# Expert tiles of a routed feed-forward: SiLU after the gate half, four tiles a loop turn, and spaced row gathers on GpSimd

## The chip, the cores and the metric

The kernel runs on one core of one Trainium2 chip. The metric is the time of one execution on the device, in microseconds. The median of three runs of the kernel before is 1096.64 us (1096.44 to 1098.18).

## What is computed

The reference is a chain of four layers over 4096 tokens of 256 features, each followed by a residual sum and a layer norm: a linear-attention layer, a quantised feed-forward, a windowed attention, and a mixture of experts. Only the last is touched:

```python
scores = softmax(xt @ Wr)                      # 8 experts, xt: tokens x 256
topk_w, topk_idx = top_k(scores, 2); topk_w /= topk_w.sum()
g = silu(einsum('th,ehd->etd', xt, Wg)); u = einsum('th,ehd->etd', xt, Wu)
out_all = einsum('etd,edh->eth', g * u, Wd)    # hidden width 512
out = sum(out_all[topk_idx, tok] * topk_w) + silu(x @ Sg) * (x @ Su) @ Sd
```

The kernel computes only the two chosen experts of each token. With the inputs that the reference draws, the experts get 1063, 698, 1016, 1056, 1166, 846, 884 and 1463 rows. Cut into tiles of 128 rows these are 9, 6, 8, 9, 10, 7, 7 and 12 tiles, 68 in all; the kernel always runs NE = 71 tiles, numbered 0 to 70. The first tile of the fourth expert (number 3 when one counts from 0, as the code does) is therefore tile 9 + 6 + 8 = 23, and that of the fifth is tile 32.

## The kernel before

The program is written by hand for each engine, with semaphores between them. The layers run one after the other, with the edges overlapped. The expert tiles take about 606 to 983 us of the span; after them come the gathers of the expert outputs and the rest of the shared expert.

**TensorE** (`tile`, line 2274) does for tile i: read the place of tile i from a table in SBUF into a register (`place_of`, line 2271, a register load; the place says which expert, and in which of three SBUF slots its weights lie); transpose the hidden rows of tile i-1 (`h_transpose_e`, line 2256, recorded as L2260, four 128x128 transposes); wait until the weights of the expert are split (`w_ready`, line 2282); the gate half and the up half of tile i (`gate_up_e`, twelve matmuls of 512 columns, six for each half, since each float32 product is done as three: lines 1857 to 1859); transpose the token rows of tile i+1 (L2244); the down product of tile i-1 (`down_e`, twelve matmuls of 256 columns). All twelve matmuls of gate and up are told by one increment of `e_gu`. Tiles 5 to 66 run in a hardware loop of two tiles a turn (line 2312), the others are written out. The first tile of a turn reads two places, its own and that of the tile before.

**ScalarE** (line 806 on) does for tile i: copy the transposed hidden rows of tile i-1 (`heh`, L789), SiLU of the gate half (`gs`, L784), copy the transposed rows of tile i+1 (`xeh`, L779), and issue the load of the rows of tile i+3 from `tokens_by_expert`; before one load in four it waits until the group with these rows has been written.

**VectorE** (line 1808 on): the low part of the hidden rows of i-1 (`hel`, L1798), the product of SiLU and up half (`hb`, `hidden_e`, L1794), the low part of the rows of i+1 (`xel`, L1788), and the copy of the output of i-1 (`ye`, L1806), which the SP queue stores.

**GpSimd** (line 1014 on) does three things in one written order. It gathers token rows by expert: 17 groups, group 0 with 2 tiles, groups 1 to 15 with four and group 16 with three (tiles 68 to 70). One indirect DMA fetches the 128 rows of a tile (`fetch`, L983), then `keep` writes the group before to `tokens_by_expert` (L990). It loads the weights of an expert (`load_expert`, L1009, 1536 KB), and for experts 3 and up it first waits for the tiles that used the slot. And it splits the weights of an expert into a high and a low part, either whole (`split_expert`, L967 and L969, 128x3072 each) or in 12 parts (`split_part`, 128x512, L975 and L978 in turn) between the fetches. When the last part is done, `w_ready` rises. The weights of experts 0 and 1 are split by ScalarE and VectorE before.

The order is: fetch tiles 0 to 5; load expert 2; groups 0 and 1; groups 2 to 7 with the parts of expert 2, one part after every second fetch; group 8; load expert 3; group 9; wait for that load; groups 10 and 11 with a part of expert 3 after every fetch (eight parts); groups 12 and 13 with a part after every second fetch (four parts); groups 14 to 16; load expert 4; then whole splits. The gathers of the expert outputs at the end (L1043) each have a 128x28 sum behind them (L1047, `pause`) in six of the eight chunks.

Of the kernel before, what the change touches and what calls it, by code (L numbers as in the profile page):

```python
# [8 lines left out]
ALU = mybir.AluOpType  # L9
# [3 lines left out]
P = 128  # L13
# [27 lines left out]
E = 8  # L41
EH = 512
EW = 2 * KD * EH + EH // P * D
SLOT = 2 * EW
NE = 2 * NT + E - 1
TOKEN_0 = T // 2
DIRECT = 6
GROUPS = ((DIRECT, 8),) + tuple((i, min(i + 4, NE)) for i in range(8, NE, 4))
# [19 lines left out]
def wait(eng, sem, n):  # L68

    if not isinstance(n, int) or n > 0:  # L70
        eng.wait_ge(sem, n)
# [22 lines left out]
def build(nc, cst, xT, x, wqkvgT, wave_cols, bias_cols, coupling_rows, woutT, bout, wgu_rows, wd_rows, wqk_T, wo_rows, bo, wr, experts, out):  # L94
    ctx = ExitStack()
    with ctx:
        place = {"at": 0, "top": 0}

        def sb(name, shape, dt=F32):
            size = 2 if dt in (BF16, F16) else 4  # L100
            for s in shape[1:]:
                size *= s
            t = nc.alloc_sbuf_tensor_at(name, shape, dt, offset=base + place["at"])
            place["at"] += (size + 31) // 32 * 32
            place["top"] = max(place["top"], place["at"])
            return t
# [15 lines left out]
        zrow = sb("zrow", [P, D])  # L122
# [134 lines left out]
        ohr = sb("ohr", [P, NT * E], F32R)  # L257
# [150 lines left out]
        def _(act):  # L408
# [366 lines left out]

            def x_high_e(i, h):
                act.wait_ge(e_t, i + 1)
                wait(act, e_gu, i - 1)
                act.activation(xeh[:, h].rearrange("p a c -> p (a c)"), PS[:, h, 0:D], ACT.Copy).then_inc(e_xhi, 1)  # L779

            def silu_e(i, h):
                act.wait_ge(e_gu, i + 1)
                wait(act, e_hb, i - 1)
                act.activation(gs[:, h], PS[:, 2], ACT.Silu).then_inc(e_si, 1)  # L784

# [9 lines left out]
            def tile(i, h, groups=None, first=False, final=False):  # L795
# [3 lines left out]
                if not final:  # L799
                    x_high_e(i + 1, 1 - h)  # L800
                    if not isinstance(i, int) or DIRECT <= i + 3 < NE:
                        if groups is not None:
                            act.wait_ge(d_rows, 16 * groups)
                        rows(i + 3, 1 - h)

            x_high_e(0, 0)
            tile(0, 0, first=True)
            for i in range(1, 5):
# [18 lines left out]
            at = 4 * (NCH - 1) + 2  # L827
# [3 lines left out]
        def _(pool):  # L831
# [139 lines left out]
            def split_part(e, n):  # L971
                place_, half, cols = (e + 2) % SLOTS, n % 2, slice(n // 2 * 2 * D, (n // 2 + 1) * 2 * D)
                hi, lo, raw = (t[:, cols].rearrange("p (n d) -> p n d", d=D) for t in (hi_of[place_], lo_of[place_], raw_of[place_]))
                if half == 0:
                    pool.tensor_tensor(hi, raw, zrow[:, :].unsqueeze(1).to_broadcast([P, 2, D]), ALU.add).then_inc(high_part, 1)  # L975
                else:
                    pool.wait_ge(high_part, PARTS // 2 * (e - 2) + n // 2 + 1)
                    last_ = pool.tensor_tensor(lo, raw, hi.bitcast(F32), ALU.subtract)  # L978
                    if n == PARTS - 1:
                        last_.then_inc(w_ready, 1)  # L980

            def fetch(out_, i, done):
                pool.indirect_dma_start(out=out_, out_offset=None, in_=XD,  # L983
                                        in_offset=bass.IndirectOffsetOnAxis(ap=token_of[:, i:i + 1], axis=0)).then_inc(done, 16)

            def keep(g):
                first, end = GROUPS[g]
                pool.wait_ge(d_stage[g % 2], 16 * sum(GROUPS[n][1] - GROUPS[n][0] for n in range(g % 2, g + 1, 2)))
                wait(pool, d_rows, 16 * g)
                pool.dma_start(XS[first * P:end * P].rearrange("(n p) d -> p n d", p=P), stages[g % STAGES][:, 0:end - first]).then_inc(d_rows, 16)  # L990

            def gather_tokens(first, end, split=None, part=0, every_=2):
                for g in range(first, end):
                    if g >= STAGES:
                        pool.wait_ge(d_rows, 16 * (g - STAGES + 1))
                    for n, i in enumerate(range(*GROUPS[g])):
                        fetch(stages[g % STAGES][:, n], i, d_stage[g % 2])
                        if split is not None and n % every_ == every_ - 1:
                            split_part(split, part)
                            part += 1  # L1000
                    if g > 0:
                        keep(g - 1)

            def load_expert(e):
                if e >= SLOTS:
                    used = pool.value_load(cum_tiles[0:1, e - SLOTS:e - SLOTS + 1], min_val=1, max_val=NE)
                    pool.wait_ge(e_dn, used)
                    pool.tensor_tensor(freed[:], zrow[:, 0:4], zrow[:, 0:4], ALU.add)
                pool.dma_start(raw_of[(e + 2) % SLOTS][:], experts[e]).then_inc(d_raw2, 16)  # L1009
# [13 lines left out]
            pool.wait_ge(d_dn, 2 * AHEAD)  # L1023
            pool.wait_ge(d_raw2, 16)
            gather_tokens(2, 8, split=2)
            gather_tokens(8, 9)
            load_expert(3)
            gather_tokens(9, 10)
            pool.wait_ge(d_raw2, 16 * 2)
            gather_tokens(10, 12, split=3, every_=1)  # L1030
            gather_tokens(12, 14, split=3, part=8)
            gather_tokens(14, len(GROUPS))
            load_expert(4)
            keep(len(GROUPS) - 1)
            loaded(4)
# [41 lines left out]
        def _(dve):  # L1077
# [62 lines left out]
            for cos_, _, turns in TABLES:  # L1140
                dve.tensor_scalar(cos_[:].bitcast(U32), turns[:].bitcast(U32), 0x7FFFFFFF, None, ALU.bitwise_and).then_inc(turns_done, 1)
# [647 lines left out]
                                  xeh[:, h].rearrange("p a c -> p (a c)").bitcast(F32), ALU.subtract).then_inc(e_xlo, 1)  # L1789

            def hidden_e(i, h):
                dve.wait_ge(e_si, i + 1)
                wait(dve, e_ht, i - 1)
                dve.tensor_tensor(hb[:, h], PS[:, 3], gs[:, h], ALU.mult).then_inc(e_hb, 1)  # L1794
# [55 lines left out]
            at = 4 * last + 3  # L1850
# [3 lines left out]
        def _(pe):  # L1854
            def three(out_, wh, wl, vh, vl, first, last_):

                pe.matmul(out_, wh, vh, start=first, stop=False)  # L1857
                pe.matmul(out_, wh, vl, start=False, stop=False)  # L1858
                return pe.matmul(out_, wl, vh, start=False, stop=last_)  # L1859
# [387 lines left out]
            def gate_up_e(i, h, base_):  # L2247
                pe.wait_ge(e_xlo, i + 1)
                wait(pe, e_hb, i)
                for w in range(2):  # L2250
                    for k in range(KD):
                        at, lo = (bass.ds(base_ + i * EW + (w * KD + k) * EH, EH) for i in range(2))
                        mm = three(PS[:, 2 + w], xeh[:, h, k], xel[:, h, k], EWs[:, at], EWs[:, lo], k == 0, k == KD - 1)
                mm.then_inc(e_gu, 1)

            def h_transpose_e(i, h):
                pe.wait_ge(e_hb, i + 1)
                wait(pe, e_hlo, i - 1)
                for j in range(4):
                    t = pe.transpose(PS[:, 4 + h, j * P:(j + 1) * P], hb[:, h, j * P:(j + 1) * P], ident)  # L2260
                t.then_inc(e_ht, 1)

            def down_e(i, h, base_):
                pe.wait_ge(e_hlo, i + 1)
                wait(pe, e_y, i - 1)
                for j in range(4):
                    at, lo = (bass.ds(base_ + i * EW + 2 * KD * EH + j * D, D) for i in range(2))
                    mm = three(PS[:, 6 + h, 0:D], heh[:, h, j], hel[:, h, j], EWs[:, at], EWs[:, lo], j == 0, j == 3)
                mm.then_inc(e_dn, 1)

            def place_of(i):
                return pe.value_load(of_tile[0:1, bass.ds(i, 1)], min_val=0, max_val=SLOTS * E - 1)

            def tile(i, h, before=None, first=False, final=False):
                place = place_of(i)
                expert, at = place % E, place // E * SLOT
                if not first:
                    if before is None:
                        before = place_of(i - 1)
                        before = before // E * SLOT  # L2280
                    h_transpose_e(i - 1, 1 - h)
                pe.wait_ge(w_ready, expert + 1)
                gate_up_e(i, h, at)
                if not final:
                    x_transpose_e(i + 1, 1 - h)
                if not first:
                    down_e(i - 1, 1 - h, before)
                return at

# [16 lines left out]
            at = tile(0, 0, first=True)  # L2306
            pe.wait_ge(d_add, 2 * AHEAD)
            at = tile(1, 1, at)
            at = tile(2, 0, at)
            at = tile(3, 1, at)  # L2310
            tile(4, 0, at)
            with pe.Fori(2, (NE - 5) // 2) as r:
                at = tile(2 * r + 1, 1)
                tile(2 * r + 2, 0, at)
            at = tile(NE - 4, 1)
            for i in range(NE - 3, NE):
                at = tile(i, i % 2, at, final=i == NE - 1)
            h_transpose_e(NE - 1, 0)
            pe.wait_ge(d_xlo, AHEAD + 1)
# [92 lines left out]
```

## Time and profile before

| | us |
|---|---|
| median of 3 runs | 1096.64 |
| the profiled execution | 1101.61 |
| its span in the trace | 1099.7 |
| TensorE busy | 1032.2 (94%) |
| VectorE busy | 764.7 (70%) |
| ScalarE busy | 489.6 (45%) |
| GpSimd busy | 442.0 (40%) |

The profiled execution is one run, and 5.0 us over the median. Its span starts with the first recorded work; 1.9 us of the execution lie around it. "PE" is TensorE, "PEld" its weight loads, "PEldq" the sequencer that issues both; "DVE" is VectorE, "ACT" ScalarE, "POOL" GpSimd. A row in order of time gives the start, the duration, the engine and line, and the operation with output and inputs; the bracket behind it is how long the engine had been idle and what released it ("issue": nothing that the profile shows). The rows of one line give count, duration in ns (least, median, most) and first and last start. The chain that ended last lies on TensorE for 53% of the span.

### The profile page before, as it was taken

The numbers are of one execution on the slowest core, as the hardware profiler recorded it, in microseconds if no ns is written. First come the engines' busy times: TensorE is split into PE (matmuls) and PEld (weight loads), VectorE is DVE, ScalarE is ACT, GpSimd is POOL, SyncE is SP. The second block draws the span as 40 slices with busy tenths as digits, with TensorE's granted clock in tenths as the row PEclk, the third lists the DMA queues.
The fourth block names the chain that finished last, engine by engine and source line by source line (L and its number), as shares of the span: only waits on it lengthen the run. The fifth ranks groups of instructions, "written<-read, shape, count | busy, mean of one in ns | idle before, by whom it ended". The sixth has DMA issues, their size and how long they took to land.

```text
span 1099.7 us, 19315 instructions
## 1 busy us (share of the span) xinstructions
PE 1032.2 (94%) x5960; PEld 901.9 (82%) x5961; DVE 764.7 (70%) x1290; ACT 489.6 (45%) x914; POOL 442.0 (40%) x445
## 2 busy tenths in 40 slices
PE   6898997799999999999999999989999999999994
PEld 5676776799999998999988787878888888888883
DVE  7988998899999987787878343333444444347886
ACT  6745755774344444666751222222322222233326
POOL 1000201555544446322100787975633200018886
PEclk9999998999999999999999999999999999999997
DMA  8100000010000000311250557464413111213335
GB/s 315 70 32 20 1 29 1 1 35 1 0 0 0 0 1 1 120 40 39 64 205 6 187 172 242 141 183 160 156 52 107 56 48 54 70 58 108 123 106 191
DMA packets 41350, 87.83 MB, mean 80 GB/s; under 512 B 5970, under 2 KB 27732, under 8 KB 39892
## 3 DMA queue, kind: packets, MB, share of 16 engines
q0 software_dynamic: 9696, 35.66, 10.5%
q1 hardware_dynamic: 20804, 39.20, 10.0%
q10 hardware_dynamic: 10800, 12.32, 3.6%
q8 instruction: 29, 0.48, 0.2%
q14 instruction: 21, 0.17, 0.0%
HBM read 57.80 MB, written 29.36 MB: 79 GB/s over the span
## 4 chain that ended last, share of the span: by engine, by line
PE 53%; DVE 19%; DVEq 10%; POOL 8%; issue 5%; ACT 4%; DMA 1%; ACTq 0%; POOLq 0%
PE PS L1857 14%; PE PS L1859 13%; PE PS L1858 13%; POOL gathered L1043 6%; PE PS L2260 3%; PE PS L2012 2%; DVEq L1433 2%; DVEq L1280 2%; POOL pause L1047 1%; DVEq L1447 1%; PE PS L2244 1%; DVE hx L1292 1%; PE PS L1910 1%; DVEq L1293 1%; DVE qinv L1283 1%
## 5 line engine op out<-in xcount | busy, mean ns | idle before, releaser
L1794 DVE TENSOR_TENSOR hb<-PS,gs 128x512 f32<-128x512 f32 x71 | 49.1, 692 | 154.0 <-ACT gs L784 143.4
L1043 POOL DMA_INDIRECT gathered<-expert_outputs,pos x64 | 66.7, 1043 | 139.5 <-DMA expert_outputs<-ye 127.2
L1857 PE MATMUL PS<-EWs,xeh 128*128 x284 | 119.8, 422 | 0.0
L784 ACT ACTIVATE gs<-PS 128x512 f32<-128x512 f32 x71 | 42.5, 598 | 162.3 <-PE PS L1859 154.0
L1859 PE MATMUL PS<-EWs,xel 128*128 x284 | 112.5, 396 | 0.0
L1858 PE MATMUL PS<-EWs,xeh 128*128 x284 | 111.8, 394 | 0.0
L1857 PE MATMUL PS<-WGh,bxh 128*128 128x352 f32 x256 | 88.0, 344 | 13.4 <-DVE hv L1427 10.5
L2012 PE MATMUL PS<-WD,htf 128*128 128x256 f32 x384 | 88.5, 380 | 1.6 <-ACT htf L573 1.5
L1857 PE MATMUL PS<-EWs,heh 128*128 x284 | 85.7, 302 | 3.9 <-issue 3.9
L789 ACT ACTIVATE heh<-PS 128x512 fp32r<-128x512 f32 x71 | 42.5, 598 | 104.4 <-PE PS L2260 86.9
L1798 DVE TENSOR_TENSOR hel<-PS,heh 128x512 fp32r<-128x512 f32 x71 | 49.1, 691 | 55.0 <-ACT heh L789 46.3
L1858 PE MATMUL PS<-WGl,bxh 128*128 128x352 f32 x256 | 85.3, 333 | 0.0
L1859 PE MATMUL PS<-WGh,bxl 128*128 128x352 f32 x256 | 85.2, 333 | 0.0
L2012 PEld LDWEIGHTS PS<-WD,htf 128*128 128x128 f32 x384 | 71.2, 190 | 10.9 <-ACT htf L573 2.5
L1858 PE MATMUL PS<-EWs,heh 128*128 x284 | 80.1, 282 | 0.0
L1859 PE MATMUL PS<-EWs,hel 128*128 x284 | 80.0, 282 | 0.0
L865 POOL TENSOR_TENSOR bq<-bx,qsc 128x512 f32<-128x512 f32 x16 | 19.6, 1226 | 117.9 <-DVE bx L1294 117.9
L1857 PEld LDWEIGHTS PS<-EWs,xeh 128*128 128x128 f32 x284 | 53.9, 190 | 16.0 <-issue 0.6
L1857 PEld LDWEIGHTS PS<-WGh,bxh 128*128 128x128 f32 x256 | 50.2, 196 | 17.2 <-issue 11.9
L1859 PEld LDWEIGHTS PS<-EWs,xel 128*128 128x128 f32 x284 | 53.7, 189 | 10.5
L1858 PEld LDWEIGHTS PS<-EWs,xeh 128*128 128x128 f32 x284 | 53.9, 190 | 9.4
L1857 PEld LDWEIGHTS PS<-EWs,heh 128*128 128x128 f32 x284 | 53.5, 188 | 4.7 <-issue 4.6
(387 smaller groups left out, 3013.5 us busy)
## 6 DMA issues: line engine op xcount, KB each, us to landing
raw_of<-experts POOLq DMA_DIRECT2D x6, 1536.0 KB
expert_outputs<-ye SPq DMA_DIRECT2D x71, 128.0 KB
xe<-tokens_by_expert ACTq DMA_DIRECT2D x65, 128.0 KB
xraw<-xT SPq DMA_DIRECT2D x8, 512.0 KB, 4.1
X<-x SPq DMA_DIRECT2D x1, 4096.0 KB, 13.3
tokens<-X SPq DMA_DIRECT2D x8, 512.0 KB, 3.1
y<-X SPq DMA_DIRECT2D x7, 512.0 KB
raw_of<-experts SPq DMA_DIRECT2D x2, 1536.0 KB, 9.5
```

The lines of the kernel that those rows point to most:

```text
L784: act.activation(gs[:, h], PS[:, 2], ACT.Silu).then_inc(e_si, 1)
L789: act.activation(heh[:, h].rearrange("p a c -> p (a c)"), PS[:, 4 + h], ACT.Copy).then_inc(e_hhi, 1)
L1043: pool.indirect_dma_start(out=gathered[c][:, j, t], out_offset=None, in_=YS, in_offset=bass.IndirectOffsetOnAxis(ap=pos[:, j, 4 * c + t:4 ...
L1280: dve.drain()
L1433: dve.drain()
L1794: dve.tensor_tensor(hb[:, h], PS[:, 3], gs[:, h], ALU.mult).then_inc(e_hb, 1)
L1798: dve.tensor_tensor(hel[:, h].rearrange("p a c -> p (a c)"), PS[:, 4 + h], heh[:, h].rearrange("p a c -> p (a c)").bitcast(F32), ALU.subtr ...
L1857: pe.matmul(out_, wh, vh, start=first, stop=False)
L1858: pe.matmul(out_, wh, vl, start=False, stop=False)
L1859: return pe.matmul(out_, wl, vh, start=False, stop=last_)
L2012: mm = pe.matmul(PS[:, 7, i * D:(i + 1) * D], htf[:, i, k], WD[:, k], start=k == 0, stop=k == FT - 1)
L2260: t = pe.transpose(PS[:, 4 + h, j * P:(j + 1) * P], hb[:, h, j * P:(j + 1) * P], ident)
```

## The change

On TensorE, `e_gu` now rises twice a tile, after the gate half and after the up half; ScalarE's SiLU waits for the first, VectorE's product for the second. The transposes of the hidden rows of tile i-1 come ahead of the reading of the place of tile i, and the place of tile i-1, where it has to be read again, is read ahead of the down product. The loop takes four tiles a turn (tiles 5 to 64), and tiles 65 to 70 are written out.

On GpSimd, groups 10 to 15 all carry parts of expert 3, one after every second fetch (12 parts in 24 fetches). In groups 8, 9 and 16 each fetch is followed by a drain and a 128x128 sum of zeros. The order of groups and loads is otherwise the same.

```diff
--- before.py
+++ after.py
@@ -775,11 +775,11 @@
 
             def x_high_e(i, h):
                 act.wait_ge(e_t, i + 1)
-                wait(act, e_gu, i - 1)
+                wait(act, e_gu, 2 * i - 2)
                 act.activation(xeh[:, h].rearrange("p a c -> p (a c)"), PS[:, h, 0:D], ACT.Copy).then_inc(e_xhi, 1)
 
             def silu_e(i, h):
-                act.wait_ge(e_gu, i + 1)
+                act.wait_ge(e_gu, 2 * i + 1)
                 wait(act, e_hb, i - 1)
                 act.activation(gs[:, h], PS[:, 2], ACT.Silu).then_inc(e_si, 1)
 
@@ -989,15 +989,18 @@
                 wait(pool, d_rows, 16 * g)
                 pool.dma_start(XS[first * P:end * P].rearrange("(n p) d -> p n d", p=P), stages[g % STAGES][:, 0:end - first]).then_inc(d_rows, 16)
 
-            def gather_tokens(first, end, split=None, part=0, every_=2):
+            def gather_tokens(first, end, split=None, part=0, paced=False):
                 for g in range(first, end):
                     if g >= STAGES:
                         pool.wait_ge(d_rows, 16 * (g - STAGES + 1))
                     for n, i in enumerate(range(*GROUPS[g])):
                         fetch(stages[g % STAGES][:, n], i, d_stage[g % 2])
-                        if split is not None and n % every_ == every_ - 1:
+                        if split is not None and n % 2 == 1:
                             split_part(split, part)
                             part += 1
+                        if paced:
+                            pool.drain()
+                            pool.tensor_tensor(ohr[:, 0:P], zrow[:, 0:P], zrow[:, 0:P], ALU.add)
                     if g > 0:
                         keep(g - 1)
 
@@ -1023,13 +1026,12 @@
             pool.wait_ge(d_dn, 2 * AHEAD)
             pool.wait_ge(d_raw2, 16)
             gather_tokens(2, 8, split=2)
-            gather_tokens(8, 9)
+            gather_tokens(8, 9, paced=True)
             load_expert(3)
-            gather_tokens(9, 10)
+            gather_tokens(9, 10, paced=True)
             pool.wait_ge(d_raw2, 16 * 2)
-            gather_tokens(10, 12, split=3, every_=1)
-            gather_tokens(12, 14, split=3, part=8)
-            gather_tokens(14, len(GROUPS))
+            gather_tokens(10, 16, split=3)
+            gather_tokens(16, len(GROUPS), paced=True)
             load_expert(4)
             keep(len(GROUPS) - 1)
             loaded(4)
@@ -1789,6 +1791,7 @@
                                   xeh[:, h].rearrange("p a c -> p (a c)").bitcast(F32), ALU.subtract).then_inc(e_xlo, 1)
 
             def hidden_e(i, h):
+                dve.wait_ge(e_gu, 2 * i + 2)
                 dve.wait_ge(e_si, i + 1)
                 wait(dve, e_ht, i - 1)
                 dve.tensor_tensor(hb[:, h], PS[:, 3], gs[:, h], ALU.mult).then_inc(e_hb, 1)
@@ -2251,7 +2254,7 @@
                     for k in range(KD):
                         at, lo = (bass.ds(base_ + i * EW + (w * KD + k) * EH, EH) for i in range(2))
                         mm = three(PS[:, 2 + w], xeh[:, h, k], xel[:, h, k], EWs[:, at], EWs[:, lo], k == 0, k == KD - 1)
-                mm.then_inc(e_gu, 1)
+                    mm.then_inc(e_gu, 1)
 
             def h_transpose_e(i, h):
                 pe.wait_ge(e_hb, i + 1)
@@ -2272,18 +2275,18 @@
                 return pe.value_load(of_tile[0:1, bass.ds(i, 1)], min_val=0, max_val=SLOTS * E - 1)
 
             def tile(i, h, before=None, first=False, final=False):
+                if not first:
+                    h_transpose_e(i - 1, 1 - h)
                 place = place_of(i)
                 expert, at = place % E, place // E * SLOT
-                if not first:
-                    if before is None:
-                        before = place_of(i - 1)
-                        before = before // E * SLOT
-                    h_transpose_e(i - 1, 1 - h)
                 pe.wait_ge(w_ready, expert + 1)
                 gate_up_e(i, h, at)
                 if not final:
                     x_transpose_e(i + 1, 1 - h)
                 if not first:
+                    if before is None:
+                        before = place_of(i - 1)
+                        before = before // E * SLOT
                     down_e(i - 1, 1 - h, before)
                 return at
 
@@ -2309,11 +2312,12 @@
             at = tile(2, 0, at)
             at = tile(3, 1, at)
             tile(4, 0, at)
-            with pe.Fori(2, (NE - 5) // 2) as r:
-                at = tile(2 * r + 1, 1)
-                tile(2 * r + 2, 0, at)
-            at = tile(NE - 4, 1)
-            for i in range(NE - 3, NE):
+            with pe.Fori(0, (NE - 7) // 4 - 1) as r:
+                at = tile(4 * r + 5, 1)
+                for i in range(6, 9):
+                    at = tile(4 * r + i, i % 2, at)
+            at = tile(NE - 6, 1)
+            for i in range(NE - 5, NE):
                 at = tile(i, i % 2, at, final=i == NE - 1)
             h_transpose_e(NE - 1, 0)
             pe.wait_ge(d_xlo, AHEAD + 1)
```

## Rows read from the trace of the kernel before

**Rows 1.** Busy time by stretch: PE, PEld, DVE, ACT, POOL, then PEclk, DMA share, GB/s
```profile
185.90:192.70 6.80, 6.09 (x21) 6.12 (x22) 5.88 (x6) 4.38 (x19) 0.69 (x1) 0.50 0.00 1
...
985.00:1050.00 65.00, 64.97 (x369) 56.81 (x368) 49.17 (x100) 22.74 (x35) 57.40 (x84) 1.00 0.38 115
```

**Rows 2.** TensorE in order of time, around its idle stretches
```profile
186.61 0.63 PE L1857 MATMUL PS<-WGh,bxh 128*128 128x352 f32 x1 [5.86 <-DVE hv L1427]
...
686.63 0.65 PE L2260 MATMUL PS<-C,hb 128*128 128x128 f32 x4 [1.88 <-issue]
...
688.62 0.63 PE L1858 MATMUL PS<-EWs,xeh 128*128 x1
...
731.26 0.50 PE L1857 MATMUL PS<-EWs,xeh 128*128 x1
...
737.43 0.38 PE L1857 MATMUL PS<-EWs,heh 128*128 x1 [2.92 <-issue]
```

**Rows 3.** The hidden rows' transposes (L2260), four to a tile, in four windows
```profile
L2260 PEld LDWEIGHTS PS<-C,hb x92: 137/140/145, 611.8 to 731.0; 128*128 128x128 f32 x92
...
L2260 PE MATMUL PS<-C,hb x172: 271/273/476, 611.8 to 837.3; 128*128 128x128 f32 x172
...
L2260 PEld LDWEIGHTS PS<-C,hb x145: 137/141/145, 756.0 to 938.0; 128*128 128x128 f32 x145
...
L2260 PE MATMUL PS<-C,hb x17: 271/273/275, 953.1 to 973.0; 128*128 128x128 f32 x17
```

**Rows 4.** GpSimd in order of time: groups, split parts, and the loads of experts
```profile
628.53 1.00 POOL L983 DMA_INDIRECT Hh<-tokens,token_of  x1 [0.31 <-issue]
...
634.51 1.29 POOL L978 TENSOR_TENSOR EWs<-raw_of,EWs 128x512 fp32r<-128x512 f32 x1
...
670.06 1.00 POOL L983 DMA_INDIRECT Hh<-tokens,token_of  x1 [0.30 <-issue]
...
675.76 0.59 POOL L1009 DMA_DIRECT2D raw_of<-experts  x1
...
685.67 0.97 POOL L983 DMA_INDIRECT Hl<-tokens,token_of  x1 [3.40 <-DMA raw_of<-experts]
...
721.25 1.30 POOL L978 TENSOR_TENSOR EWs<-raw_of,EWs 128x512 fp32r<-128x512 f32 x1
...
773.95 6.80 POOL L967 TENSOR_TENSOR EWs<-raw_of,zrow 128x3072 fp32r<-128x3072 f32 x1 [6.49 <-DMA raw_of<-experts]
780.98 6.79 POOL L969 TENSOR_TENSOR EWs<-raw_of,EWs 128x3072 fp32r<-128x3072 f32 x1 [0.23 <-issue]
...
837.07 0.20 POOL L1008 TENSOR_TENSOR freed<-zrow 128x4 f32<-128x4 f32 x1 [28.66 <-PE PS L1859]
```

**Rows 5.** GpSimd in order of time, 1040 us: a short sum, then a gather
```profile
1040.08 0.24 POOL L1047 TENSOR_TENSOR pause<-zrow 128x28 f32<-128x28 f32 x1
1040.47 0.97 POOL L1043 DMA_INDIRECT gathered<-expert_outputs,pos  x1 [0.16 <-issue]
```

**Rows 6.** All engines in order of time, from tile to tile at 850 us
```profile
850.17 0.39 PE L1859 MATMUL PS<-EWs,xel 128*128 x1
...
850.68 0.60 ACT L784 ACTIVATE gs<-PS 128x512 f32<-128x512 f32 x1 [2.31 <-PE PS L1859]
...
851.31 0.69 DVE L1794 TENSOR_TENSOR hb<-PS,gs 128x512 f32<-128x512 f32 x1 [2.21 <-ACT gs L784]
...
852.05 0.66 PE L2260 MATMUL PS<-C,hb 128*128 128x128 f32 x4
...
852.56 0.50 PE L1857 MATMUL PS<-EWs,xeh 128*128 x1
```

**Rows 7.** TensorE's sequencer at lines 2272 and 2282, 849.5 to 852.4 us
```profile
L2272 PEldq TENSOR_LOAD <-of_tile x1: 302/302/302, 850.3 to 850.3; - x1
L2272 PEldq SEQ_ASSERT  x1: 18/18/18, 850.9 to 850.9; - x1
...
L2282 PEldq FUSED_REGOPS  x1: 86/86/86, 852.1 to 852.1; - x1
```

## Prediction

> **What bounds the kernel now.** I read the page first (TensorE busy 94%, and most of the chain that ended last), then the busy time by stretch, then TensorE and GpSimd in order of time over the expert tiles, and last the line of the hidden rows' transposes, whose count tells which tile TensorE has reached.
>
> The transposes come four to a tile, those of tile i-1 ahead of the gate of tile i. From 756.0 to 938.0 us lie 36 tiles of 182.0 / 36 = 5.056 us; that is the pace of the loop. The written-out tiles near the end take 19.8 / 4 = 4.95 us, on rows rounded to a tenth [rows 3]. Earlier the pace is worse: 92 transposes are 23 tiles, so the group at 730.7 us is that of tile 22, and the 22 tiles from 611.8 us take 118.9 us where the pace asks 111.2. The 172nd transpose is the last of tile 42, at 837.3 us (its group began some 0.4 earlier); 16 tiles of 5.056 back, the group at 756.0 us is that of tile 26. From tile 22 to tile 26 go 25.3 us where the pace asks 20.2. So 7.7 us are lost ahead of tile 23 and 5.1 behind it. The losses are idle stretches of TensorE (1.88 and 2.92 us) and a slow clock behind them: the 512-column matmul at 688.62 us lasts 0.63 us, against the 0.39 of an ordinary one [rows 2, 6]. They fall where GpSimd's indirect DMAs follow each other. In the last stage, where a 0.24 us sum stands behind each gather, TensorE is busy for 64.97 of 65 us [rows 1, 5]. The spacing thus has a real target.
>
> **GpSimd, part by part.** The weights of expert 3 must be split before tile 23 (9 + 6 + 8 tiles come first). The counts can be checked: expert 7's load waits for the 42 tiles of the first five, and the wait ends at 837.07 us, as the last transposes of tile 42 run, behind the down product of tile 41 [rows 3, 4]. Before, the last part ends at 721.25 + 1.30 = 722.6 us, and the gate of tile 23 starts at 731.26 [rows 2, 4]. The margin is 8.7 us. The change spends it:
>
> The spaced gathers of group 8 delay expert 3's load. An unspaced fetch takes 1.00 + 0.30 us. The new 128x128 sum is not in the trace; between 0.24 us for 28 columns and 1.29 for 512 a straight line gives 0.46. The drain is between nothing and the 0.23 us idle ahead of the second whole add, which stands behind one. A spaced fetch is then 0.97 + 0.16 + 0.46 + 0.23 = 1.8 us, at least the 0.97 + 0.16 + 0.24 = 1.4 of the last stage and at most 2.2. I take 1.8, since drain and sum are both of these kinds. Four of them add 2.2 us, and the load goes out at 678.2 instead of 675.76. Before, it was in by 685.67, 9.9 us later; a load with no gathers beside it took about 7.1 (6.49 idle and 0.56 of issue). With 9.9 it is in at 688.1; group 9, spaced, ends about 687.5. So group 10 starts at 688.1 us (684.5 to 690) instead of 685.67 [rows 4, 5].
>
> From there, parts come after every second fetch. Five such groups take 670.06 - 628.53 = 41.5 us, 8.31 each, and the second part of a group ends 634.51 + 1.29 - 628.53 = 7.3 us after the group's start [rows 4]. Six groups: 5 x 8.31 + 7.3 = 48.8 us. The last part ends at 688.1 + 48.8 = **736.9 us** (733.3 to 739), 14.3 later than before.
>
> TensorE would be at tile 23 before that: at 731.26 us if nothing were gained, and some 5 us sooner if the spacing removes its idle time. It waits on `w_ready` for 5.6 to 11 us. Queued behind that wait on its one sequencer are the gate and up of tile 23, the transposes of tile 24's rows and the down product of tile 22; ScalarE, VectorE and the SP store wait for these. Everything won ahead of tile 23, by spacing or pace, is swallowed. Against before, tile 23 starts 736.9 - 731.26 = **+5.6 us** (+2.0 to +7.7).
>
> The wait also costs clock. After an idle stretch of 5.86 us TensorE ran at 0.50, the lower of its levels (1.2 instead of 2.4 GHz), for 6.8 us, in which it was busy for 6.1: some 3.0 us lost [rows 1, 2]. After 1.88 us idle, about 3.4 us were slow by the matmul durations around 688.62: 1.7 lost. Here I take **+2.4 us** (+1.0 to +3.1).
>
> Behind tile 23 the gain is real: of the 5.1 us lost between tiles 22 and 26, I take back **-4.5 us** (-2.5 to -5.1). The parts of groups 14 and 15, the spaced group 16 and the later load leave no row of bare fetches. Group 16 adds 3 x 0.5 us on GpSimd, under the split of expert 4 (load at about 745, 10 us of load, 14 of splitting: ready by 770, needed for tile 32 near 782). Its cover is 12 us; gone, each us would be one.
>
> **The tile itself.** Before, 0.51 us pass from the start of the last gate-and-up matmul to the SiLU (850.17 to 850.68), 0.63 to the product, 0.74 to the transposes and 0.51 to the next gate (852.56): 2.39 us, and the other 2.67 of the pace are the gate and up matmuls [rows 3, 6]. SiLU on the gate half takes its 0.63 us off this round: it runs beside the up half's six matmuls. But the register load moves behind the transposes. Before, the sequencer did it at 850.2 to 850.9, under the down product. It then stood at the transposes: the next register work (L2282) is stamped 852.1, the transposes' own start, not 851.0 [rows 7]. So the load cannot start ahead of the end of the transposes' wait, and the gate behind it comes 0.78 us later (about 0.1 of index, 0.30 of load, 0.4 of checks and arithmetic, 850.2 to 851.0). The round grows by 0.78 - 0.63 = 0.15, to 5.21 us. Off this come the loop's branch and second place, which stretched each second tile before and now lie between the down product and the wait, on nothing; the written-out tiles (4.95) bound what they and the loop cost together at 0.10. A second wait on VectorE may add up to 0.1, and a load that stays hidden would give 4.95. I take 5.08, a little under the middle of 4.95 and 5.3, since the loop's cost leaves for certain. Some 47 tiles follow tile 23: 47 x (5.08 - 5.056) = **+1.1 us** (-5 to +8).
>
> The load took 0.30 us here [rows 7]. The Trainium skill ("DMA: Bandwidth & Descriptors", latency and other measured facts) states a floor of about 600 ns for `tensor_load`. By that figure the exposed load would add 0.3 us a tile, 14 us more; the trace disagrees, and I go by the trace.
>
> **Sum.** 5.6 + 2.4 - 4.5 + 1.1 = +4.6 us. The terms come from one profiled execution of 1101.61 us (span 1099.7), 5.0 over the median. If part of that excess is TensorE's idle time, the gain is smaller and the wait longer in an unprofiled run, so I don't scale the sum down: 1096.64 + 4.6 = 1101.2 us.
>
> **Rivals.**
> (a) The register load stays hidden because waiting transposes don't hold the sequencer. Then the tiles run at 4.95: 47 x -0.106 = -5.0 instead of +1.1, and with the wait 5.6 + 2.4 - 4.5 - 5.0 = -1.5, 1095.1 us, no change. The stamps of rows 7 speak against it. The Trainium skill ("Advanced Engine Details and Errata", sequencer and instruction queues) speaks for it: engine instructions wait in a queue for their semaphores while others are read.
> (b) Faster: expert 3 is ready early. A fetch pitch of 1.4 and a 7 us load put the last part at 733.3 us. With (a)'s pace: 2.0 + 1.0 - 5.1 - 5.0 = -7, 1089.5 us. It is faster for any last part up to about 734.5. Against: the 9.9 us that this load took.
> (c) The spacing does not do what it says: the idle time is TensorE's own, or the load's traffic. Then nothing comes back behind tile 23: 5.6 + 2.4 + 1.1 = +9, 1105.7 us. The last stage's full TensorE speaks against, though its work is looser.
>
> **Chances.** Forecast 0.53, (a) 0.20, (b) 0.12, (c) 0.15. A change under 0.2% (2.2 us) cannot be told from none. Faster: (b) and a little of (a), 0.16. Same: most of (a) and the low end of the forecast, 0.24. Slower: 0.60. The range leaves out the ends of (b) and of (c): 1092.5 to 1107.5.
>
> **What would show it.** An idle stretch of TensorE of 6 to 11 us ahead of tile 23's gate, ended by the last L978 part near 737 us; a slow clock behind it; expert 3's load going out near 678; no idle stretch over 0.5 us elsewhere from 671 us on; L2272's load stamped behind the transposes, and the pace from 756 to 938 us at 5.03 to 5.15. I am wrong if TensorE does not wait there, or if the last part ends before 731 us.

## The result and the profile after

The changed kernel takes 1130.34 us (median of 4 runs, 1129.7 to 1131.65) against 1096.59 beside it: a ratio of 1.0302 (95% interval 1.0289 to 1.0316), 33.75 us slower. Forecast were 1101.2 us and a range of 1092.5 to 1107.5. The profiled execution took 1131.65 us, with a span of 1129.7 against 1099.7.

The page of the changed kernel, its head (busy us, share of the span, instructions):

```profile
span 1129.7 us, 19363 instructions
PE 1028.4 (91%) x5960; PEld 897.4 (79%) x5961; DVE 768.5 (68%) x1290; ACT 497.4 (44%) x914; POOL 445.9 (39%) x456
```

TensorE's work is nearly the same (1028.4 us busy, 1032.2 before); the span around it has grown. Who TensorE waited for, 560 to 1040 us (us in total, times, longest):

```profile
PE PS L1860 <- POOL EWs L978: 32.9, 1, 32.9
PE PS L1860 <- issue: 2.7, 8, 0.7
```

One wait of 32.9 us, for a split part of GpSimd. Before, no row of this view named GpSimd. In order of time, TensorE and GpSimd at its end:

```profile
758.21 1.27 POOL L978 TENSOR_TENSOR EWs<-raw_of,EWs 128x512 fp32r<-128x512 f32 x1
...
759.88 0.79 PE L1860 MATMUL PS<-EWs,xeh 128*128 x1 [32.91 <-POOL EWs L978]
760.46 0.63 PE L1861 MATMUL PS<-EWs,xeh 128*128 x1
```

This is tile 23's gate, held by expert 3's last part, which ends at 759.5 us (722.6 before, [rows 4]). The matmuls behind it last 0.63 us, as those at the low clock in [rows 2]. The stretch behind the wait (span, then busy PE, PEld, DVE, ACT, POOL, clock, DMA share, GB/s), and the transposes that follow it:

```profile
759.90:764.50 4.60, 4.60 (x11) 3.63 (x12) 0.00 (x0) 0.60 (x1) 1.33 (x2) 0.50 0.53 145
```

```profile
766.39 0.46 PEld L2263 LDWEIGHTS PS<-C,hb 128*128 128x128 f32 x4
```

The granted clock is 0.50, the lower level (1.2 instead of 2.4 GHz). Where GpSimd's time went, in order of time, from the start of group 8 to that of group 10:

```profile
669.75 1.00 POOL L983 DMA_INDIRECT Hh<-tokens,token_of  x1 [0.30 <-issue]
675.33 0.40 POOL L1003 TENSOR_TENSOR ohr<-zrow 128x128 fp32r<-128x128 f32 x1 [4.58 <-issue]
676.00 0.97 POOL L983 DMA_INDIRECT Hh<-tokens,token_of  x1 [0.28 <-issue]
678.92 0.40 POOL L1003 TENSOR_TENSOR ohr<-zrow 128x128 fp32r<-128x128 f32 x1 [1.95 <-issue]
...
688.16 0.57 POOL L1012 DMA_DIRECT2D raw_of<-experts  x1 [0.29 <-issue]
689.03 1.02 POOL L983 DMA_INDIRECT Hh<-tokens,token_of  x1 [0.30 <-issue]
696.99 0.40 POOL L1003 TENSOR_TENSOR ohr<-zrow 128x128 fp32r<-128x128 f32 x1 [6.94 <-issue]
...
710.78 1.00 POOL L983 DMA_INDIRECT Hl<-tokens,token_of  x1 [0.30 <-issue]
```

and the line of the drains (count; ns least, median, most):

```profile
L1002 POOLq DRAIN  x11: 3032/4239/9342, 666.0 to 771.8; - x11
```

The engine is idle not behind the sum but between fetch and sum: the drain does not end when the fetch has been issued. The drain's own durations say too much, because its stamp can begin ahead of the fetch: the first starts at 666.0 us and its fetch only at 669.75. What it costs is read from the idle time ahead of the eleven sums, 36.5 us together, 1.9 to 6.9 each. The longest, 6.94 us, stands behind the fetch that had the 1536 KB load of expert 3 ahead of it; the DMA engines were busy for 0.90 of the time up to that sum and 0.27 behind it:

```profile
689.00:697.00 8.00, 7.54 (x46) 6.41 (x46) 3.54 (x8) 2.18 (x4) 1.03 (x2) 1.00 0.90 299
697.00:702.00 5.00, 4.89 (x31) 4.19 (x30) 2.08 (x5) 1.59 (x3) 1.60 (x3) 1.00 0.27 66
```

The two other first fetches of a group, behind the store of a group of rows, come next (4.58 and 4.74 us). That the drain lasts until transfers are done is the reading that fits these rows; which transfers it waits for was not tested. The two spaced groups take 710.78 - 669.75 = 41.0 us, against 15.6 before and the 18.0 forecast.

The pace, in the transposes' line, for 36 tiles from tile 26's transposes on, and TensorE's sequencer at one tile:

```profile
L2263 PEld LDWEIGHTS PS<-C,hb x145: 137/141/141, 782.0 to 968.3; 128*128 128x128 f32 x145
...
L2275 PEldq TENSOR_LOAD <-of_tile x1: 302/302/302, 854.0 to 854.0; - x1
L2275 PEldq SEQ_ASSERT  x1: 18/18/18, 854.6 to 854.6; - x1
...
L2282 PEldq FUSED_REGOPS  x1: 86/86/86, 854.7 to 854.7; - x1
```

```profile
852.65 0.39 PE L1862 MATMUL PS<-EWs,xel 128*128 x1
...
853.08 0.69 DVE L1797 TENSOR_TENSOR hb<-PS,gs 128x512 f32<-128x512 f32 x1 [1.87 <-PE PS L1862]
...
854.52 0.60 PE L2263 MATMUL PS<-C,hb 128*128 128x128 f32 x4
...
855.22 0.50 PE L1860 MATMUL PS<-EWs,xeh 128*128 x1
```

The pace is 186.3 / 36 = 5.17 us (5.056 before, [rows 3]). The product starts 0.43 us behind the last matmul's start and ends at 853.77; the register load is stamped 854.0, behind it, not under the down product as in [rows 7]; the gate follows at 855.22. From the product's end to the gate are 1.45 us, with the load and its arithmetic in them; before it was 0.56 [rows 6]. From the last gate-and-up matmul's start to the gate are 855.22 - 852.65 = 2.57 us, against 2.39 before.

### The profile page after: what moved, and what is told of

Same layout as the page of the kernel before. It is cut to its first block, busy times and chain, and to the rows that moved or that the text cites. A ratio compares the mean times of both kernels' runs of the same rounds, so it can differ in the third digit from the quotient of the medians.

```text
span 1129.7 us, 19363 instructions
## 1 busy us (share of the span) xinstructions
PE 1028.4 (91%) x5960; PEld 897.4 (79%) x5961; DVE 768.5 (68%) x1290; ACT 497.4 (44%) x914; POOL 445.9 (39%) x456
## 4 chain that ended last, share of the span: by engine, by line
PE 41%; DVE 19%; POOL 14%; DVEq 10%; issue 8%; ACT 5%; DMA 1%; POOLq 1%; ACTq 0%
PE PS L1860 11%; PE PS L1862 10%; PE PS L1861 10%; POOL gathered L1045 4%; PE PS L2015 2%; PE PS L2263 2%; POOL even_rows L983 2%; DVEq L1435 2%; DVEq L1282 2%; POOL Hh L983 1%; POOL EWs L978 1%; POOL Hl L983 1%; POOL EWs L975 1%; DVEq L1449 1%; DVE hx L1294 1%
## 5 line engine op out<-in xcount | busy, mean ns | idle before, releaser
L1860 PE MATMUL PS<-EWs,xeh 128*128 x284 | 119.7, 422 | 39.8 <-POOL EWs L978 32.9
L779 ACT ACTIVATE xeh<-PS 128x256 fp32r<-128x256 f32 x71 | 27.4, 386 | 87.4 <-PE PS L2247 85.3
```

## Experiments

All kernels compute the full result. The kernel before was run beside each set, and its median is given with it, since it differs between sets: 1096.59 beside the changed kernel, 1097.56 beside the first three runs below (chip 6), 1087.64 beside the next four (chip 12) and 1088.18 beside the last four (chip 7). The kernels that wait long at tile 23 do not get those 10 us: the change without drains takes 1105.37 us on chip 12, the one without drains and sums 1104.32 on chip 6. So across sets neither times nor ratios can be compared to better than the 10 us (0.9%), and conclusions rest on kernels of one set where there are two.

**No drain and no sum.** The changed kernel with

```diff
-            gather_tokens(8, 9, paced=True)
+            gather_tokens(8, 9)
...
-            gather_tokens(9, 10, paced=True)
+            gather_tokens(9, 10)
...
-            gather_tokens(16, len(GROUPS), paced=True)
+            gather_tokens(16, len(GROUPS))
```

> The changed kernel with neither drain nor sum behind the fetches of groups 8, 9 and 16; the twelve parts stay spread over groups 10 to 15. Theory D: expert 3's load is out at 675.8 us, the last part ends at 685.7 + 48.8 = 734.5 us, TensorE waits 1 to 7 us at tile 23, and idle stretches of 1 to 3 us come back in groups 8, 9 and 16: 1102 to 1108 us. Rival S: over 1120 us. If this is faster than the run without the drain, the sum buys nothing.

1104.32 us, ratio 1.0060 (1.0043 to 1.0077). The waits of TensorE, 600 to 1000 us:

```profile
PE PS L1860 <- POOL EWs L978: 5.9, 1, 5.9
```

The spacing costs 26 of the 33.7 us, by medians of two sets in which the kernel before is within 1 us. The spread of the parts costs a wait of 5.9 us: the last part ends at 730.30 + 1.27 = 731.6 us in this trace (734.5 was given; group 8 starts 2 us earlier than assumed). Groups 8 and 9 were bare, and the idle stretches that were expected there did not come back: TensorE is busy for 49.15 of the 50 us from 670 on.

**The tiles' part alone.** The TensorE, ScalarE and VectorE hunks of the change, GpSimd's code as before.

> The TensorE, ScalarE and VectorE part of the change alone, GpSimd as before. Theory P (the register load behind the transposes lengthens each tile's round): 5.18 us from 756 to 938 us as in the changed kernel, against 5.056 before, over some 66 tiles 8 us, less what slack it gives against idle stretches: 1101 to 1106 us. Rival Q (the slower pace is GpSimd's doing, the splits or the later load): pace 5.06 or less, 1094 to 1098 us.

1100.23 us, ratio 1.0025 (1.0016 to 1.0035). The pace is P's, so it is not GpSimd's doing:

```profile
L2261 PEld LDWEIGHTS PS<-C,hb x145: 137/141/142, 750.8 to 937.0; 128*128 128x128 f32 x145
```

186.2 / 36 = 5.17 us. The time is a little under the range given, so the longer round costs less than 8 us. From the transposes of tile 0 to those of tile 22 go 115.9 us, 3.0 less than before [rows 3], although the pace is slower: less is lost to idle time there. That the longer round leaves slack for it is a guess; from tile 22 to tile 26 go 25.4 us, as before.

**The place ahead of the transposes again.** The kernel of the last run with

```diff
 def tile(i, h, before=None, first=False, final=False):
+    place = place_of(i)
+    expert, at = place % E, place // E * SLOT
     if not first:
         h_transpose_e(i - 1, 1 - h)
-    place = place_of(i)
-    expert, at = place % E, place // E * SLOT
```

> As the run before this one, but the place is read ahead of the transposes again, so that SiLU on the gate half and the four-tile loop act alone. Theory P: the register load is under the down product again, the SiLU's 0.63 us are off the round, and the tiles are bound by TensorE's own work: pace 4.95 to 4.98 us, 66 x -0.1 = 6.6 us less than before, 1088 to 1092 us. Rival Q or a bound elsewhere: pace 5.03 or more, 1095 us or more.

1080.43 us, ratio 0.9844 (0.9827 to 0.9860): 20 us less than the run above by two moved lines, and 8 us under the range given. Pace and one tile's turn in this kernel:

```profile
L2261 PEld LDWEIGHTS PS<-C,hb x145: 137/141/141, 744.0 to 917.5; 128*128 128x128 f32 x145
```

```profile
853.68 0.69 DVE L1795 TENSOR_TENSOR hb<-PS,gs 128x512 f32<-128x512 f32 x1 [1.50 <-PE PS L1860]
...
854.84 0.28 PE L1860 MATMUL PS<-EWs,hel 128*128 x1
854.96 0.49 PE L2261 MATMUL PS<-C,hb 128*128 128x128 f32 x3
```

The pace is 173.5 / 36 = 4.82 us. The product ends at 854.37, the transposes start 0.12 us behind the last down matmul: nothing but TensorE's own work sets the tile. The prediction and theory P took 4.95 for that floor; it was too high. In this trace one long stretch of idle time is left, which ends as expert 4's load goes out (736.82 us):

```profile
736.81 0.38 PE L1858 MATMUL PS<-EWs,heh 128*128 x1 [3.01 <-DVE hel L1799]
```

**Sums without drains.** The changed kernel with (a counter `spaced = [0]` is set up in front)

```diff
-    pool.drain()
-    pool.tensor_tensor(ohr[:, 0:P], zrow[:, 0:P], zrow[:, 0:P], ALU.add)
+    at = 23 * spaced[0]
+    spaced[0] += 1
+    pool.tensor_tensor(ohr[:, at:at + 23], zrow[:, 0:23], zrow[:, 0:23], ALU.add)
```

> The changed kernel with no drain; behind each fetch of groups 8, 9 and 16 stands a sum of 23 columns, each into columns of its own, instead of the 128x128 sum into one place. Theory D (the drain waits for the landing): a spaced fetch takes about 1.4 us, the load of expert 3 is out by 677, the last part ends at 734 to 737 us, TensorE waits 7 to 11 us at tile 23; 1103 to 1108 us, as without any spacing (1104.3), since what the sums win ahead of tile 23 is lost in the wait. Rival S (the sum, not the drain, costs the time): the load goes out after 682 us and the run takes over 1112 us.

1105.37 us, ratio 1.0159 (1.0142 to 1.0176). GpSimd in order of time:

```profile
671.27 0.97 POOL L983 DMA_INDIRECT Hh<-tokens,token_of  x1 [0.16 <-issue]
672.26 0.23 POOL L1006 TENSOR_TENSOR ohr<-zrow 128x23 fp32r<-128x23 f32 x1
672.65 0.97 POOL L983 DMA_INDIRECT Hh<-tokens,token_of  x1 [0.16 <-DMA tokens_by_expert<-even_rows]
```

A spaced fetch takes 672.65 - 671.27 = 1.38 us, the 1.4 of [rows 5]. The wait is 7.1 us instead of 32.9. The sum is smaller here too, 0.23 us against 0.40 in the changed kernel; that is under 2 us over the eight fetches ahead of group 10, and the rest is the drain's. No run takes out the drain and leaves the 128x128 sum.

**Sums in the faster kernel.** Place first, SiLU on the gate half, four tiles a turn, GpSimd's order of before, and behind the fetches of groups 8, 9 and 12 to 16 a sum as above, of 9 columns.

> The place read ahead of the transposes, SiLU on the gate half and four tiles a turn (1080.4 us by itself), GpSimd in the order of before, and a sum of 9 columns, with no drain, behind every fetch of groups 8, 9 and 12 to 16. Theory B (bare fetches one behind the other are what idles TensorE): the stretch of 9.0 us from transposes to transposes at 731 to 740 us goes to under 5.5, 4 to 5 us won, 1075 to 1077 us. Rival L (the idle time comes with the row loads and stores landing late while GpSimd's DMAs are in flight, whatever their spacing by a fraction of a us): the 9 us stretch stays, 1079 to 1082 us.

1078.77 us, ratio 0.9915 (0.9899 to 0.9932). The time lies between the two ranges, and it decides nothing between B and L: the stretch at 731 to 740 us is gone, but the next run, of the same set and without the sums, has none either. What the trace shows is a 5.0 us wait on expert 3's part at tile 23, longer than in the same kernel without the sums (3.4, last run but one): the last part ends at 722.5 us here and at 719.1 there.

**Two tiles a turn.** The kernel before with (the three waits on `e_gu` in short)

```diff
-                mm.then_inc(e_gu, 1)
+                    mm.then_inc(e_gu, 1)
...
-                act.wait_ge(e_gu, i + 1)
+                act.wait_ge(e_gu, 2 * i + 1)
...
+                dve.wait_ge(e_gu, 2 * i + 2)
```

and the place of tile i-1 read ahead of the down product.

> The kernel before with SiLU on the gate half and the place of the tile before read ahead of the down product; two tiles a turn and the place ahead of the transposes as before. Theory P: most of the 0.24 us a tile of the run with the place first (4.82 against 5.056) is SiLU's 0.63 us off the round, so the pace here is 4.82 to 4.86 and the time 1080 to 1083 us. Rival R: the branch every second tile sets half of it, pace 4.9 to 4.97, 1086 to 1091 us.

1078.77 us, ratio 0.9920 (0.9903 to 0.9936). The pace over 33 tiles, 754.5 to 913.5 us, is 159.0 / 33 = 4.82 us:

```profile
L2261 PEld LDWEIGHTS PS<-C,hb x133: 137/141/141, 754.5 to 913.5; 128*128 128x128 f32 x133
```

So all of the pace is there with two tiles a turn. The time is 1.2 us under the range given, which was reckoned from a set with a slower kernel before.

**GpSimd's part alone.** The GpSimd hunks on the kernel before.

> The GpSimd part of the change alone (drains, sums, spread parts), the tiles as before. Theory D: the last part ends at 759 to 760 us as in the changed kernel, TensorE waits about 30 us at tile 23, and from there the tiles go at 5.05 instead of 5.18 us: 48 x 0.13 = 6 us less than the changed kernel, 1122 to 1126 us. If the last part ends much earlier, the tiles' part delays GpSimd through shared DMA traffic.

1125.15 us, ratio 1.0344 (1.0327 to 1.0361). TensorE's waits, and the drains:

```profile
PE PS L1859 <- POOL EWs L978: 35.1, 1, 35.1
```

```profile
L1002 POOLq DRAIN  x11: 3021/4097/9567, 664.7 to 769.4; - x11
```

GpSimd's part by itself loses 37.5 us here, so it makes all of the loss. The wait is 35.1 us where about 30 were given; the last part ends at 757.1. Beside it, in the same set, the run with sums and no drains is 19.8 us faster (1105.37), although it has the slower tiles.

**Expert 3's and 4's loads earlier.** The two-tile kernel with

```diff
-            gather_tokens(2, 8, split=2)
-            gather_tokens(8, 9)
+            gather_tokens(2, 7, split=2)
             load_expert(3)
-            gather_tokens(9, 10)
+            gather_tokens(7, 8, split=2, part=10)
+            gather_tokens(8, 9)
             pool.wait_ge(d_raw2, 16 * 2)
-            gather_tokens(10, 12, split=3, every_=1)
-            gather_tokens(12, 14, split=3, part=8)
-            gather_tokens(14, len(GROUPS))
+            gather_tokens(9, 12, split=3, every_=1)
             load_expert(4)
+            gather_tokens(12, len(GROUPS))
```

> As the run with SiLU on the gate half and two tiles a turn, and expert 3's load issued after group 6 instead of 8, its twelve parts behind the fetches of groups 9 to 11, expert 4's load after group 11 instead of 16. Theory W (in the faster tiles tile 23 is held by expert 3's last part, 2.5 us in that run's trace): the last part ends before 713 us, no wait on it at tile 23, 2 to 3 us less than that run beside it on the same chip. Rival B (bare fetches behind one another idle TensorE): groups 12 to 16 are now bare, 19 fetches in a row, and give back 2 to 5 us, so that it is not faster.

1072.03 us, ratio 0.9849 (0.9832 to 0.9865), the lowest time of all runs and 5.0 us under the best other kernel of its set (1077.03, below). GpSimd's last part, and the busy time of 670 to 760 us (span, then PE, PEld, DVE, ACT, POOL, clock, DMA share):

```profile
705.31 1.31 POOL L978 TENSOR_TENSOR EWs<-raw_of,EWs 128x512 fp32r<-128x512 f32 x1
```

```profile
670.00:760.00 90.00, 90.00 (x556) 79.48 (x556) 40.32 (x74) 29.47 (x57) 71.97 (x63) 1.00 0.59 186
```

The part ends at 706.6, ahead of tile 23 at 718, and TensorE is never idle in this stretch, though 19 bare fetches follow one another. So the wait is gone, as theory W has it, and on this chip B falls. W's 2 to 3 us could not be checked: the same two-tile kernel was not run in this set, and its ratio above, 0.9920, comes from another.

**Four tiles a turn alone.** As the place-first run, with `e_gu` once a tile and SiLU behind the whole gate and up.

> The kernel before with four tiles a turn, the place of the tile before read ahead of the down product, and SiLU behind the whole gate and up as before. Theory P: the round with the whole SiLU is about 5.0 us (2.39 us from the last matmul to the gate, 2.6 of matmuls), so the pace from tile 26 to 62 is 4.95 to 5.02, and the time 0 to 6 us under before. Rival R (branch and second place cost the pace): 4.82 to 4.86.

1082.13 us, ratio 0.9937 (0.9917 to 0.9957), pace 179.8 / 36 = 4.99 us:

```profile
L2260 PEld LDWEIGHTS PS<-C,hb x145: 137/140/145, 741.0 to 920.8; 128*128 128x128 f32 x145
```

Without the earlier SiLU the larger loop and the place of the tile before take 0.06 us off the round; with it they are hidden.

**The place first once more.**

> The run with the place first and four tiles a turn once more, to stand beside the two-tile loop and the two runs before on one chip. If four tiles a turn buy nothing, pace 4.82 and the time within 2 us of the two-tile run's ratio to before.

1077.03 us, ratio 0.9898 (0.9881 to 0.9914), pace 4.82. Its interval overlaps the two-tile run's (0.9903 to 0.9936), so four tiles a turn show no clear gain. In the first set the same kernel had 0.9844: the tiles' gain was 17 us there and is 11 here. In this set the idle stretch at 731 us is not there. TensorE now waits 3.4 us for expert 3's last part, by the view of waits:

```profile
PE PS L1858 <- POOL EWs L978: 3.4, 1, 3.4
```

**The whole change with the place first.** The two lines moved as above, on the changed kernel.

> The whole change with one thing undone: the place is read ahead of the transposes. Theory D: the last part of expert 3 still ends at 757 to 760 us, TensorE waits 37 to 41 us at tile 23, and what the faster tiles win ahead of it is lost; behind it 47 tiles at 4.82 instead of 5.18 win 17 us: 1111 to 1115 us.

1116.50 us, ratio 1.0259 (1.0236 to 1.0281), 1.5 us over the range. The wait is 42.8 us where 37 to 41 were given:

```profile
PE PS L1860 <- POOL EWs L978: 42.8, 1, 42.8
```

Tiles of 4.82 us bring TensorE to tile 23 earlier, and it waits longer (42.8 us instead of 32.9). The last part's end hardly moves (758.5 instead of 759.5). Ahead of the wait a faster tile is worth nothing. Against the run above, which differs by GpSimd's part alone, 39.5 us are lost.

## Why the prediction was wrong

The direction, the wait and its place were right; one term was mis-sized and carried the time out of the range.

**The spaced fetch: wrong.** The step that failed is "the drain is between nothing and the 0.23 us idle ahead of the second whole add". That row's drain stands between two sums; here it stands behind an indirect DMA, and GpSimd is idle for 1.9 to 6.9 us between fetch and sum. I had no row of a drain behind a DMA in flight and took the nearest as an upper bound, which nothing in it supported. A spaced fetch took 3.6 us (676.00 to 679.6) and up to 8.6 (689.03 to 697.67), where I had 1.8 and at most 2.2. Expert 3's load went out at 688.16 us instead of 678.2, and group 10 started at 710.8 instead of 688.1. (675.76 + 2.2 is 678.0, so my 678.2 was also 0.2 too high, which changes nothing.) The run with sums and no drains, where the term is 1.38 us, confirms the size: its wait is 7.1 us, in the 5.6 to 11 that I gave.

**The parts: right.** From group 10's start to the last part's end were 759.48 - 710.78 = 48.7 us, forecast 48.8.

**Tile 23's start:** 759.88 - 731.26 = +28.6 us, forecast +5.6. The 22.7 us too few at group 10 are nearly all of the difference.

**The clock: right in size.** From tile 23's gate to the next transposes went 766.39 - 759.88 = 6.5 us, where at the pace it is 5.17 - 0.70 = 4.5 (0.70 from transposes to gate, 854.52 to 855.22): 2.0 us, forecast 2.4.

**Behind tile 23: right in size, the cause not shown.** From the gate of tile 23 to the transposes of tile 26, nearly four turns, went 22.1 us, against 24.8 before; without the clock's 2.0 that is -4.7, forecast -4.5. But the run with neither drain nor sum takes 22.7 us there (731.96 to 754.65), so the spacing of group 16 gives at most some 0.5 of it. What is left may be the spread of the parts or the later tile 23 itself; no run tells them apart.

**The pace: right in kind, low in size.** 5.17 us, just over the 5.03 to 5.15 named as a sign, forecast 5.08 out of bounds of 4.95 and 5.3. The round grew by 2.57 - 2.39 = 0.18 us where I had 0.15, and the loop and the second place gave back 0.06 (four tiles a turn alone) where I took off 0.13. In the sum, 0.115 x 44 tiles are about 5 us by the pace, and the transposes of tile 70 lie 3.8 us later against those of tile 26 than before, since the unrolled tiles are slower by less. Forecast +1.1. The sum is 28.6 + 2.0 - 4.7 + 3.8 = +29.7, against 30.0 between the two spans.

**The medians** differ by 3.7 us more than the profiled executions. I had named this side: the kernel before is faster in its other runs (1096.6 against 1101.6), the changed one only by 1.3. Which stretch makes that was not shown.

**The rivals.** (a), the load that stays hidden, fell: its stamp moved behind the product, and the run with the place first shows what hiding it is worth. The Trainium skill ("Advanced Engine Details and Errata", sequencer and instruction queues) lists an engine instruction as pushed into a queue and waiting for its semaphore, and says that others can be read while a control instruction runs; that register work passes a waiting transpose it does not say; rival (a) read it so. Here an unmet wait of a transpose held the register work behind it, at 854.0 in the changed kernel as at 852.1 before. The Trainium skill's `tensor_load` floor of about 600 ns ("DMA: Bandwidth & Descriptors", latency and other measured facts) also disagrees with the row: 302 ns. (b) fell. (c) is open in part: spacing can help only where bare fetches idle TensorE. In the last two sets four runs keep bare fetches (two tiles a turn, earlier loads, four tiles alone, the place first once more), and from 620 us on none has an idle stretch over 0.5 us but the wait on expert 3's last part. Whether sums without drains remove the idle time in a set that has it was not tried.

## What to carry over

A drain behind a DMA that GpSimd issues itself is not priced by a drain between two sums: when a trace has no such row, leave the upper bound open to the transfer's whole time. Where one engine prepares what another will need at a known tile, compute both arrival times from the trace first; everything won ahead of the wait is swallowed, and the slack of that one deadline is what a reordering spends. And read a register ahead of the instruction whose wait holds the sequencer, not behind it: the same instructions in the other order took 0.35 us a tile off here.

## What the runs showed of the hardware that was not expected

A drain behind an indirect DMA kept GpSimd idle for 1.9 to 6.9 us (median 3.1), longest behind the fetch that had a 1536 KB load ahead of it; the stamps of the drains (3.0 to 9.3 us) begin earlier, some ahead of the fetch. TensorE's tile of 30 matmuls and transposes runs in 4.82 us, under the 4.95 of the written-out tiles before, once no semaphore is late. The lower clock does not follow from the length of an idle stretch alone: behind 1.88 us idle the kernel before had 0.62 from 686.6 to 691.1 us, behind 3.01 us the place-first kernel kept 1.00:

```profile
736.80:745.00 8.20, 7.62 (x49) 6.72 (x49) 3.68 (x7) 2.69 (x6) 1.39 (x3) 1.00 0.97 297
```

And the same kernel before has medians of 1097.6 and 1087.6 us on different chips; idle stretches like those of [rows 2] show in traces of the first sets and hardly in the later ones, so a gain worked out from them does not hold everywhere.
